# Routing three steps later with four record buffers, and a new order of the prologue, in a fused cross-attention and mixture-of-experts kernel

## The reference

```python
x = x + tanh(g_xattn) * attn(layernorm(x), ctx, ctx)     # 16 heads of 8, softmax over 128 keys
x = x + tanh(g_ffn)   * moe(layernorm(x))                # 8 experts, 128 -> 512 -> 128
# moe: logits = tokens @ Wg; expert = argmax; position = running count of the tokens
#      that chose this expert; a token with position >= 512 is dropped;
#      out = gate * (relu(token @ W1[e] + b1[e]) @ W2[e] + b2[e])
```

## Time and profile before

| what | value |
|---|---|
| median of 3 runs | 354.58 us (354.29 to 359.06) |
| the profiled execution | 352.81 us, of which the span from first to last instruction is 351.0 us |
| PE busy | 261.1 us (74%) |
| DVE busy | 201.8 us (57%) |
| ACT busy | 158.5 us (45%) |
| POOL busy | 173.4 us (49%) |
| mean granted clock of PE | 0.886 |

### The profile page before, as it was taken

The page is one execution under the profiler, slowest core; times in us unless marked ns, Lnnn a source line. Parts: engine busy times, 40 slices in busy tenths (PEclk is TensorE's granted clock), DMA queues, the critical chain, the costliest instruction groups (busy, mean ns, idle before and its releaser), DMA issues.

```text
span 351.0 us, 8166 instructions
## 1 busy us (share of the span) xinstructions
PE 261.1 (74%) x2960; PEld 169.0 (48%) x2960; DVE 201.8 (57%) x696; ACT 158.5 (45%) x357; POOL 173.4 (49%) x202
## 2 busy tenths in 40 slices
PE   0348698888996995996896888969331899999920
PEld 0124445545654654654654555635220366777720
DVE  6244649778895895568687597932320144544520
ACT  7253376865764763564674456551010332322100
POOL 5336724757179179238728625070462005555572
PEclk9999999999998998589899699995555699999985
DMA  2984765615244235208217111074014225664300
GB/s 79 294 222 110 229 183 149 182 32 162 64 115 129 66 91 152 63 3 230 51 29 209 43 56 64 5 200 76 30 51 130 71 64 162 186 200 142 89 37 21
DMA packets 48536, 39.26 MB, mean 112 GB/s; under 512 B 9619, under 2 KB 44072, under 8 KB 48497
## 3 DMA queue, kind: packets, MB, share of 16 engines
q1 hardware_dynamic: 44784, 28.67, 30.5%
q0 software_dynamic: 3712, 10.07, 8.6%
HBM read 13.72 MB, written 12.65 MB: 75 GB/s over the span
## 4 chain that ended last, share of the span: by engine, by line
POOL 26%; issue 26%; PE 22%; ACT 8%; DVE 7%; DMA 5%; SPq 2%; POOLq 1%; ACTq 0%; DVEq 0%
POOL rec_dram L1002 7%; POOL out_dram L1056 6%; POOL rs L982 4%; PE O L489 3%; PE X L418 3%; ACT prob L623 2%; ACT xn L615 2%; DVE negm L734 2%; POOL rec L988 2%; PE S L460 2%; POOL rec L990 2%; PE X L412 2%; PE TS L561 2%; PE X L435 2%; DMA qp<-parts_q 2%
## 5 line engine op out<-in xcount | busy, mean ns | idle before, releaser
L734 DVE TENSOR_REDUCE negm<-S 128x4 f32<-128x512 f32 x128 | 81.8, 680 | 27.5 <-PE S L460 26.5
L623 ACT ACTIVATE prob<-TS 128x512 f32<-128x512 f32 x128 | 72.0, 589 | 47.5 <-PE TS L475 47.3
L489 PE MATMUL O<-prob,vals 128*32 128x128 f32 x1024 | 58.1, 303 | 1.6 <-ACT oraw L632 1.6
L460 PE MATMUL S<-kp,qp 62*128 62x128 bf16 x512 | 33.5, 234 | 5.2 <-DVE negm L734 4.7
L1056 POOL DMA_INDIRECT out_dram<-fin,tok x32 | 31.3, 979 | 11.2 <-issue 11.2
L1002 POOL DMA_INDIRECT rec_dram<-rec,slot x32 | 31.8, 994 | 9.7 <-issue 9.7
L256 POOL TENSOR_TENSOR rest_k<-full_k,parts_k 128x512 f32<-128x512 f32 x7 | 8.1, 1155 | 53.4 <-ACT parts_k L606 53.4
L489 PEld LDWEIGHTS O<-prob,vals 128*32 128x32 f32 x1024 | 21.3, 113 | 21.7 <-issue 10.9
L975 POOL TENSOR_TENSOR fence_p<-pool_c 128x1 f32<-128x1 f32 x16 | 3.1, 194 | 56.7 <-DVE fin L955 34.3
L460 PEld LDWEIGHTS S<-kp,qp 62*128 62x128 bf16 x512 | 19.2, 100 | 23.5 <-issue 11.7
L475 PE MATMUL TS<-qp,kp 64*128 64x128 bf16 x512 | 28.9, 228 | 1.3 <-DMA qp<-mrow 1.3
(11 more groups left out here) (115 smaller groups left out, 513.1 us busy)
## 6 DMA issues: line engine op xcount, KB each, us to landing
kp<-parts_k SPq DMA_DIRECT2D x48, 128.0 KB
qp<-parts_q SPq DMA_DIRECT2D x48, 128.0 KB, 2.7
rec_dram<-zeros POOLq DMA_DIRECT2D x8, 516.0 KB
xr<-rec_dram SPq DMA_DIRECT2D x8, 260.0 KB, 2.9
c_sb<-in_ctx_dram SPq DMA_DIRECT2D x8, 256.0 KB, 4.4
out_dram<-rec SPq DMA_DIRECT2D x8, 256.0 KB
w1s<-in_L_ffn_W_dram SPq DMA_DIRECT2D x8, 256.0 KB, 3.1
w2s<-in_L_ffn_W_dram SPq DMA_DIRECT2D x8, 256.0 KB, 2.9
```

Of the source, the lines that this page charges most:

```text
L460: mm = nc.tensor.matmul(S[:, a, i * L:(i + 1) * L], qp[b][rows, h, t0:t0 + L], kp[b][rows, h, t0:t0 + L], start=True, stop=True)
L489: mm = nc.tensor.matmul(o_out[i * HV:(i + 1) * HV, u * L:(u + 1) * L], vals[G % 2][:, k, h, :], prob[n % 2][:, h * L:(h + 1) * L], start=( ...
L623: nc.scalar.activation(prob[n % 2][:, first:first + 4 * L], TS[:, a, :], ACT.Exp).then_inc(a_exp, 1)
L734: V.tensor_reduce(negm[n % 2][:, first:first + 4], S[:, a, :].rearrange("p (h k) -> p h k", k=L), AX.X, ALU.max, negate=True).then_inc(v_r ...
```

## The change

The routing tasks move: `nT` from j=1 of group g-2 to j=0 of g-3 (step 4G+9 to 4G+12 for group G), `lg` with `logits` and `route` from j=2 to j=1 (4G+10 to 4G+13), `pos` with `positions` and `place` from j=3 to j=2 (4G+11 to 4G+14), and `scatter` from 4G+11 to 4G+15. `norm2` stays at 4G+8. There are four record and slot buffers in place of three, and four steps more in the loop. `x` is loaded in eight DMAs by group in place of three; the first context load stands second in SP's queue. The statistics of groups 0 and 1 and the splits of group 0 stand ahead of the clearing of buffers and of the routing's masks. `zero_records` runs in steps 1 to 8 in place of -7 to 5. `ident_b`, which nothing reads, is gone. Parts that only replace a 3 by `RB` are left out below.

```diff
-    FIRST, LAST = -8, 4 * (NG - 1) + 11
+    FIRST, LAST = -8, 4 * (NG + 2) + 3
+    RB = 4
...
-        ident_b = sb("ident_b", [P, P], BF16)
...
-        rec = [sb(f"rec{i}", [P, GB, REC]) for i in range(3)]
+        rec = [sb(f"rec{i}", [P, GB, REC]) for i in range(RB)]
...
-            third = {2: ("lg", g - 2), 3: ("pos", g - 2)}.get(j)
+            third = {1: ("lg", g - 3), 2: ("pos", g - 3)}.get(j)
...
-            second = {1: ("nT", g - 2), 2: ("xT", g + 2), 3: ("q", g + 2)}.get(j)
+            second = {0: ("nT", g - 3), 2: ("xT", g + 2), 3: ("q", g + 2)}.get(j)
...
             sp.dma_start(x_sb[:, 0:GB, :], x_v[:, 0:GB, :]).then_inc(x_in[0], 16)
+            sp.dma_start(c_sb[0][:], ctx_v[:, 0:GB, :]).then_inc(c_in[0], 16)
...
                     if H < 3:
-                        sp.wait_ge(a_pad, H + 1)
+                        if H == 0:
+                            sp.wait_ge(a_pad, 1)
+                        else:
+                            sp.wait_ge(g_pad, H)
...
-                if loads:
+                if loads and g + 2 >= 1:
...
-                if c == -7:
-                    sp.dma_start(x_sb[:, 2 * GB:, :], x_v[:, 2 * GB:, :]).then_inc(x_in[2], 16)
+                if j == 2 and 2 <= g + 3 < NG:
+                    rows = slice((g + 3) * GB, (g + 4) * GB)
+                    sp.dma_start(x_sb[:, rows, :], x_v[:, rows, :]).then_inc(x_in[g + 3], 16)
...
-                if j == 2 and is_group(g + 2):
+                if j == (2 if g + 2 else 1) and is_group(g + 2):
                     H = g + 2
                     act.wait_ge(p_cT, H + 1)
...
-                if j == 1 and is_group(g - 2):
-                    G = g - 2
+                if j == 0 and is_group(g - 3):
+                    G = g - 3
                     act.wait_ge(p_nT, G + 1)
                     nc.scalar.activation(xn2T[:], X[:, 0, :], ACT.Copy).then_inc(a_nT, 1)
...
-                if j == 1 and is_group(g + 2):
+                if j == 1 and g + 2 == 0:
+                    normed1(0, (0, 1, 2, 3)).then_inc(a_xn, 1)
+                elif j == 1 and is_group(g + 2):
                     normed1(g + 2, (0, 1))
-                if j == 2 and is_group(g - 2):
-                    G = g - 2
+                if j == 1 and is_group(g - 3):
+                    G = g - 3
                     act.wait_ge(v_ldif, G + 1)
                     nc.scalar.activation(lexp[:], ldif[:], ACT.Exp).then_inc(a_lexp, 1)
 
-            for i in range(3):
-                nc.scalar.memzero(qp[i][:]).then_inc(a_pad, 1)
-            act.wait_ge(s_bias, 96)
-            nc.scalar.activation(tg[:], gains[:], ACT.Tanh).then_inc(s_tanh, 1)
-            act.wait_ge(s_vset, 1)
+            nc.scalar.memzero(qp[0][:]).then_inc(a_pad, 1)
...
             def moments2(G):
                 dve.wait_ge(v_st2, GB * G + GB)
+                if G >= 1:
+                    dve.wait_ge(g_xn2, G)
...
+            def ones_in(i):
+                V.memset(kp[i][:].rearrange("p h n -> p (h n)").bitcast(F32), ONES_B).then_inc(v_pad, 1)
+
+            def weights():
+                dve.wait_ge(s_wqkv, 16)
+                V.tensor_copy(wk_dh[:].rearrange("p (a d h) -> p a d h", a=2, d=HD),
+                              wqkv[:, D:2 * D].rearrange("p (a h d) -> p a d h", a=2, d=HD))
+                V.tensor_copy(wq_dh[:].rearrange("p (a d h) -> p a d h", a=2, d=HD),
+                              wqkv[:, 0:D].rearrange("p (a h d) -> p a d h", a=2, d=HD)).then_inc(s_vset, 1)
...
+                if c == -7:
+                    weights()
                 if is_batch(c):
                     top(c, 1)
-                if j == 2 and is_group(g - 2):
-                    logits(g - 2)
-                if j == 3 and is_group(g - 2):
-                    positions(g - 2)
-                if j == 2 and is_group(g - 2):
-                    route(g - 2)
-                if j == 3 and is_group(g - 2):
-                    place(g - 2)
-                if j == 2 and g + 2 == 0:
+                if j == 1 and is_group(g - 3):
+                    logits(g - 3)
+                    route(g - 3)
+                if j == 2 and is_group(g - 3):
+                    positions(g - 3)
+                    place(g - 3)
+                if c == -6:
                     split(dve, V, 1, 0)
-                if j == 0 and is_group(g + 2):
+                    moments1(1)
+                if c == -5:
+                    gathered1(1)
+                    split(dve, V, 0, 0)
+                    offset1(1)
+                if j == 0 and is_group(g + 2) and g + 2 != 1:
                     moments1(g + 2)
-                if j == 1 and is_group(g + 2):
+                if j == 1 and is_group(g + 2) and g + 2 != 1:
                     offset1(g + 2)
-
-
-            for i in range(3):
-                V.memset(kp[i][:].rearrange("p h n -> p (h n)").bitcast(F32), ONES_B).then_inc(v_pad, 1)
+                if c == -7:
+                    dve.wait_ge(s_bias, 64)
+                    V.tensor_scalar(bq_s[:], bqk[:, 0:1], SCALE, None, ALU.mult).then_inc(s_vset, 1)
+                    ones_in(1)
+
+
+            ones_in(0)
...
                 if c == -4:
+                    ones_in(2)
+                    V.tensor_copy(before_b[:], cst[:, P:2 * P])
+                    V.memset(ones_b[:], 1.0)
+                    V.memset(mask[:], 0.0)
+                    V.memset(seen[:], 0.0)
...
                 if j == 0 and is_group(g - 2):
                     norm2(g - 2)
-                if j == 0 and g - 3 == NG - 2:
-                    scatter(NG - 2)
                 if j == 1 and is_group(g + 2):
                     root(g + 2, mv1, rs1, v_mv1, g_e1).then_inc(g_rs1, 1)
-                for i in {-7: (0, 1), 0: (2,), 1: (3,), 2: (4,), 3: (5,), 4: (6,), 5: (7,)}.get(c, ()):
+                if c == -7:
+                    for i in (1, 2):
+                        G_.memset(qp[i][:].rearrange("p h n -> p (h n)").bitcast(F32), 0.0).then_inc(g_pad, 1)
+                for i in ((c - 1,) if 0 <= c - 1 < ZEROED else ()):
                     zero_records(i)
-                if j == 1 and is_group(g + 1):
+                if j == 1 and is_group(g + 1) and g + 1 != 0:
                     split(pool, G_, 0, g + 1)
...
-                if j == 3 and is_group(g - 2) and g - 2 != NG - 2:
-                    scatter(g - 2)
+                if j == 3 and is_group(g - 3):
+                    scatter(g - 3)
```

More of the change, by code:

```diff
@@ L148, in flamingo_kernel @@
         base = sb("base", [P, GB])
-        slot = [sb(f"slot{i}", [P, GB], U32) for i in range(3)]
+        slot = [sb(f"slot{i}", [P, GB], U32) for i in range(RB)]
         w1s = [sb(f"w1s{i}", [P, F]) for i in range(2)]
@@ L264, in zeros_sent @@
         def zeros_sent(p):
-            return 16 * len(range(p, ZEROED, 3))
+            return 16 * len(range(p, ZEROED, RB))
         def run_steps(step_fn):
@@ L371, in load_xr @@
                 sp.dma_start(xr[e % 2][:], rec_v[e][:, :, D:REC]).then_inc(xr_in[e % 2], 16)
-            for p in range(3):
-                sp.wait_ge(sent[p], zeros_sent(p) + 16 * GB * len(range(p, NG, 3)))
+            for p in range(RB):
+                sp.wait_ge(sent[p], zeros_sent(p) + 16 * GB * len(range(p, NG, RB)))
             for e in range(2):
@@ L391, in _ @@
                 load_xr(e)
-            for p in range(3):
-                sp.wait_ge(x1_out[p], 16 * len(range(p, NG, 3)))
+            for p in range(RB):
+                sp.wait_ge(x1_out[p], 16 * len(range(p, NG, RB)))
             for p in range(2):
@@ L652, in step @@
                         first_part(1, 0)
-                if j == 2 and is_group(g + 2):
+                if j == 2 and is_group(g + 2) and g + 2 != 0:
                     normed1(g + 2, (2, 3)).then_inc(a_xn, 1)
+                if c == -5:
+                    act.wait_ge(s_vset, 2)
+                if c == -4:
+                    act.wait_ge(s_gain, 32)
+                    nc.scalar.activation(tg[:], gains[:], ACT.Tanh).then_inc(s_tanh, 1)
                 if is_batch(c - 2):
@@ L759, in residual @@
                 dve.wait_ge(g_xb, n // GB + 1)
-                G, row1 = n // GB, rec[n // GB % 3][:, n % GB, D:2 * D]
-                if n % GB == 0 and G >= 3:
-                    dve.wait_ge(sent[G % 3], zeros_sent(G % 3) + 16 * GB * (G // 3))
-                    dve.wait_ge(x1_out[G % 3], 16 * (G // 3))
+                G, row1 = n // GB, rec[n // GB % RB][:, n % GB, D:2 * D]
+                if n % GB == 0 and G >= RB:
+                    dve.wait_ge(sent[G % RB], zeros_sent(G % RB) + 16 * GB * (G // RB))
+                    dve.wait_ge(x1_out[G % RB], 16 * (G // RB))
                 row = x_sb[:, bass.ds(n, 1), :].rearrange("p o d -> p (o d)")
@@ L992, in scatter @@
             def scatter(G):
-                p = G % 3
+                p = G % RB
                 if G == 0:
-                    for q in range(3):
+                    for q in range(RB):
```

(4 more changed lines are left out.)

52 lines of the change are left out of this document (19 added, 33 removed).

## The result

Measured in 20 runs each: 361.69 us median after (355.58 to 364.46) against 354.59 us before (351.57 to 359.13), a ratio of 1.0119 with an interval of 1.0076 to 1.0162. All ratios here are taken over the runs within 1.5% of the fastest of their kernel, and so differ from the quotient of the medians, which is 1.020 here. The changed kernel was 1.2% slower where I had forecast 6% faster. That is not all.

| comparison | before, us | changed, us | ratio, 95% interval |
|---|---|---|---|
| the first | 354.6 | 361.7 | 1.012, 1.008 to 1.016 |
| again | 349.6 | 340.6 | 0.971, 0.965 to 0.977 |
| again_2 | 349.5 | 342.3 | 0.976, 0.968 to 0.983 |
| again_3 | 356.8 | 359.4 | 1.019, 1.009 to 1.029 |
| again_4 | 356.6 | 361.0 | 1.012, 1.005 to 1.018 |

The account below looks back on a forecast made before the run. PE was taken to stand idle 23.0 us at `nT` for POOL's late `norm2`, with DVE waiting for POOL's `root`. Terms -6.1 -1.0 -3.85 -1.9 -5.0 -3.95 = -21.8 us gave 333 us against 354.58, range 326 to 342.

Parts of the forecast that it names:

- Steps 8 to 15: Loop cycles before scatters: `lg` and `route` into idle time, first scatter moved to step 15; -3.85 us for both cycles.
- split of k to split of k: Sign in the loop: time between successive starts of POOL's split of k, near 23.3, 23.3, 26, 26 us.
- Idle PE ahead of L430: Sign in the loop: PE's 23.0 us of waiting at `nT` for POOL's `norm2` would be gone until the end.
- Prologue and traffic: Start of kernel and DMA: first scores at 24.5 us, gaining 6.1 us, and DMA traffic gaining 1.0 us.
- The prologue's own term: Before the loop: statistics need only group 0's `x` and constants, so first scores come 6.1 us earlier.
- The traffic term: DMA traffic: no clearing transfer in step 0 beside `mrow`; -1.0 us, between -1.7 and +1.
- the scatter's 2.85: Steps 8 to 15: group 0's scatter moves out to step 15, so its old cycle loses 2.85 us.
- Steps 16 to 23: Loop cycles with scatters ahead of `root`: stall at `nT` goes but `nm` stays late; -1.9 us, between -5.4 and +5.
- What is late next is `nm`: Steps 16 to 23: `nm` stays as late once the `nT` stall goes; two cycles lose only 0.5 us each.
- Steps 24 to 31: Late loop cycles without `root`: nothing replaces the stalls at `nT`; -5.0 us.
- Last steps, to the first read: End of loop: a 3.45 us stall goes, clock may stay up, work behind `at` grows 1.0 us; sum -3.95 us.
- the wait only moves: Rival, whole loop: `nm`, q parts and longer end eat every gain after the prologue; 347.5 us, chance 0.06.

Follow-up runs that it names:

- again: The changed kernel unaltered, measured and profiled a second time against the kernel before: 0.971.
- again_2: The changed kernel unaltered, measured once more against the kernel before: 0.976.
- again_3: The changed kernel unaltered, measured again against the kernel before: 359.38 us, 1.019.
- again_4: The changed kernel unaltered, measured again against the kernel before: 361.01 us, 1.012.
- prologue_only: The kernel before with only the new prologue, loads by group and places of zeroing; old routing steps and three record buffers kept: 345.21 us, 0.986.
- route_step2: The changed kernel with `logits` and `route` one step later, and positions, place and scatter likewise: 341.34 us, 0.972.
- both_late: The changed kernel with `logits` and `route` one step later and `norm2` moved behind `root` and the addition to x_sb: 333.23 us, 0.941.
- scatters_after: The changed kernel with eight record buffers and all scatters behind the last step: 366.23 us, 1.023.
- both_hole_2: The both_late kernel with the scatter moved into POOL's idle stretch one cycle later, measured a second time: 350.48 us, 0.991.

## Why the prediction was wrong

The failed step is in *Steps 8 to 15*: "`route` goes with it, into DVE's wait of 3.05 us." I took a wait for an empty place. DVE waited there for `rs`, with `nm` to come next; `route` stands ahead of `nm` in DVE's order, and I never asked how long it takes. From `cand` at 103.85 to the end of `mask` at 107.24 it took 3.39 us in step 13, where no scatter makes `rs` late.

Three of its instructions took 0.97 to 1.13 us beside POOL's split of q (1.15 to 1.20 each); in step 17 of again `mask`, off that split, took 0.19. The Trainium skill, page "SBUF — State Buffer", section "SBUF: two separate sides", has it that VectorE with two SBUF inputs and GpSimd take a shared port pair in turn, one blocking the other for a whole instruction. This case's rows agree: `nm` takes 1.10 beside the split (135.22) and 0.15 where it comes as the split has ended (107.17), while `route`'s reductions with one input stay at 0.17 to 0.20. Not every POOL instruction does it: that `mask` of 0.19 us ran inside POOL's `rs` of 1.01 us (134.18).

The prediction named its own sign: split of k to split of k near 23.3, 23.3, 26 and 26 us. In again the splits of k start at 66.96, 92.58, 121.65, 150.11 and 179.61, so the cycles took 25.6, 29.1, 28.5 and 29.5. Idle PE ahead of L430 (L435 in the changed kernel) did go, as forecast.

By terms, from again's row of the table, which has no stretches (forecast in brackets):

- Prologue and traffic, to step 8: -5.7 (-7.1). The prologue's own term held, -6.5 at step 1 for -6.1, and prologue_only keeps it to the end. The traffic term did not: from step 1 to 8 again loses 0.8 where -1.0 was forecast, and no row showed the 1.7 us that it was bounded by.
- Steps 8 to 15: +3.2 (-3.85). The failed step. route_step2, with `route` out of the way, has -1.0, and both_late -2.8: the scatter's 2.85 come in part.
- Steps 16 to 23: +0.4 (-1.9). "What is late next is `nm`" held, and was the answer for every cycle with a `root`; both_late, in which neither `norm2` nor `route` holds `nm`, gains 6.3 us here (-8.6 to -14.9).
- Steps 24 to 31: -2.4 (-5.0). "No `root` any more, so nothing takes the place of the stalls" was right for step 25 (step 26 starts at -6.1), but `route` of that step, with three instructions of 0.89 to 1.08 us beside `norm2` and a split, then holds up `mrow`, and PE waits 2.50 us for it in step 26.
- Last steps, to the first read: -4.8 (-3.95). The size held; the tail from `at` of batch 31 to the read took 21.3 us (237.22 to 258.55), where 20.3 was forecast.

Sum -9.3 for -21.8. On the scale of the prediction (354.58) that is 345 us, between the forecast of 333 and the rival *the wait only moves* (347.5) and nearer to the rival. Its mechanism was the true one inside the loop: what was gained there was eaten by `nm`, and in step 26 by `mrow`; only the gain of the last steps came. I gave it 0.06 because steps 24 to 31 have no `root`; but it had three cycles before those to act in, and `route` took its place in them. That both_late came to 0.941 (0.952 when measured again), near the forecast's ratio of 0.939, is no merit of the forecast: it needed two edits that the change does not have. Two sums of the prediction are slightly off and change nothing: 20.75 less 19.3 is 1.45, not 1.3, and the terms of steps 24 to 31 add up to 5.2, given as 5.0.

The first result's further 19 us at the first read (+9.9 against -9.3) were foreseen by no rival. They come with the stretches, which scatters_after shows to need scatters in the loop, and with a clock that is lower in the same traces (0.812 against 0.857 in again). I read the kernel before from one execution that had none, though the runs shown reached 359.06; the spread of its runs was a warning that I passed over. What the stretches are is not settled. The chip alone is not the cause: again, without them, and again_3 and again_4, with them, ran on the same one. The six traces with stretches (that of scatters_after has them behind the loop) hold 4634 to 4842 recorded semaphore events, the fourteen without 5542 to 5679, for nearly the same instructions. So missing events and stretches go together, and "remote" may only mean that the releasing event is not in the trace; the times of the runs show that the delay is real. The Trainium skill, page "NOTIFIC — the notification-queue block", section 7.1, has it that a full queue of notification records either loses records or stalls the engine that writes them, by its setting; the missing events fit a loss of records, and no run here shows whether an engine was stalled by it, nor what of the machine differed between comparisons.

## What to carry to other kernels

A wait in an engine's queue is no room for new work unless the new work stands behind the waiting instruction, or is shorter than what is left of the wait; give it a duration, with the neighbour beside which it will run. Where two engines wait for one late third, follow both chains to the instruction where they meet, and expect no gain until the last of them is moved. A wait that is taken out may also have been a buffer: with the stretches the kernel before was 7 us slower (349.5 to 356.7), the changed one 19 (341.4 to 360.2), though how much of that is the lower clock is not separated.

## What was not expected of the hardware

In three of eight comparisons, and in the others with the same program not, VectorE and ScalarE stood still in waits of 2 to 6 us while GpSimd issued indirect transfers or just after, beyond the time at which their operands were ready; the trace puts some 16 us of ScalarE's waits in a loop down to it, and ScalarE's idle time ahead of `prob` is 12.0 us longer (52.6 in again_2, 64.6 in again_4). TensorE went on longer, with short idle times for which the trace names no cause (0.38 and 0.98 us in both_hole_2 at 141.88 and 143.30). The experts, whose rows go out by indirect transfers too, had one or two such waits in each of the six traces with stretches, 2.5 to 5.1 us long, on VectorE. The eight clearing transfers from GpSimd's queue brought none. And an instruction of 4 elements a partition, `nm`, took 0.15 or 1.10 us by what GpSimd did beside it.
